# The centring of the next graph's rows moved ahead of the step's closing root, and the four diagonals of E taken by one wide product and one sum

## The reference

```python
h = jnp.maximum(_layernorm(x), 0.0)
def layer(h, params):
    u = einsum('bid,bjd->bij', h, h) / sqrt(D)
    a = softmax(u, axis=-1)
    delta = a * adjacency_matrix
    attn = delta / (sum(delta, axis=-1, keepdims=True) + 1e-10)
    hl, hs, hr = h @ wl.T + b_l, h @ ws.T + b_s, h @ wr.T + b_r
    diag_a = jnp.diagonal(attn, axis1=1, axis2=2)
    ctx = (attn * upper) @ hl + diag_a[..., None] * hs + (attn * lower) @ hr
    o = (ctx - mean(ctx)) / sqrt(var(ctx) + 1e-12) * g + beta
    return relu(o)
out = x + layer(layer(h, params[0]), params[1])
```

## Time and profile before

| what | us |
|---|---|
| median of 3 runs | 1187.16 (1187.15 to 1187.18) |
| the profiled execution | 1188.02 |
| its span, first to last instruction | 1186.3 |
| PE busy | 1169.5 (99%), 6998 matmuls |
| DVE busy | 1004.8 (85%) |
| POOL busy | 633.0 (53%) |
| ACT busy | 494.5 (42%) |

### The profile page before, as it was taken

How to read it: one execution, slowest core, us unless ns; L and a number is a source line. 1 busy time by engine, 2 the same in 40 slices (tenths; PEclk the granted TensorE clock), 3 DMA queues, 4 the chain that set the end, 5 groups by cost and what they waited for, 6 DMA issues and landing times.

```text
span 1186.3 us, 18757 instructions
## 1 busy us (share of the span) xinstructions
PE 1169.5 (99%) x6998; PEld 1157.7 (98%) x6998; DVE 1004.8 (85%) x2064; ACT 494.5 (42%) x1065; POOL 633.0 (53%) x669
## 2 busy tenths in 40 slices
PE   9999999999999999999999999999999999999997
PEld 7999999999999999999999999999999999999997
DVE  6879987799877998779997798977989779895688
ACT  5346423364343543435434343344433454335532
POOL 3676454654545555455564455654556544654347
PEclk9999999999999999999999999999999999999999
DMA  6521312013120131211312112121222113110000
GB/s 226 203 65 54 115 54 81 19 54 116 54 81 19 54 115 55 80 36 55 97 54 81 37 63 90 58 76 37 83 70 80 54 36 104 48 54 1 1 27 27
DMA packets 43483, 80.57 MB, mean 68 GB/s; under 512 B 6912, under 2 KB 24832, under 8 KB 43392
## 3 DMA queue, kind: packets, MB, share of 16 engines
q1 hardware_dynamic: 43104, 78.98, 20.0%
q10 hardware_dynamic: 288, 0.39, 0.1%
HBM read 66.72 MB, written 12.64 MB: 67 GB/s over the span
## 4 chain that ended last, share of the span: by engine, by line
PE 54%; DVE 20%; POOL 10%; issue 10%; ACT 4%; DMA 1%; DVEq 0%; POOLq 0%
PE u_ps L337 9%; PE u_ps L339 9%; PE u_ps L338 9%; PE rot_ps L339 8%; PE rot_ps L338 8%; PE rot_ps L337 8%; POOL dg L957 4%; POOL hw_lo L945 4%; DVE et_lo L682 3%; DVE e_sb L677 3%; DVE xt_sb L665 3%; DVE proj L710 2%; DVE z L747 2%; DVE z L755 2%; ACT e_sb L515 2%
## 5 line engine op out<-in xcount | busy, mean ns | idle before, releaser
L945 POOL TENSOR_TENSOR hw_lo<-proj,hw_hi 128x384 fp32r<-128x384 f32 x256 | 283.1, 1126 | 242.3 <-ACT hw_hi L525 242.3
L337 PE MATMUL rot_ps<-w_hi,ht_hi 128*128 128x384 f32 x1152 | 389.3, 338 | 0.0
L339 PE MATMUL rot_ps<-w_hi,ht_lo 128*128 128x384 f32 x1152 | 385.4, 335 | 0.0
L338 PE MATMUL rot_ps<-w_lo,ht_hi 128*128 128x384 f32 x1152 | 385.2, 334 | 0.0
L338 PEld LDWEIGHTS rot_ps<-w_lo,ht_hi 128*128 128x128 f32 x1152 | 216.6, 188 | 0.0
L337 PEld LDWEIGHTS rot_ps<-w_hi,ht_hi 128*128 128x128 f32 x1152 | 216.5, 188 | 0.0
L339 PEld LDWEIGHTS rot_ps<-w_hi,ht_lo 128*128 128x128 f32 x1152 | 216.3, 188 | 0.0
L500 ACT ACTIVATE u_off<-u_ps 128x128 f32<-128x128 f32 (+1 forms) x128 | 42.4, 332 | 395.6 <-PE u_ps L339 395.4
L525 ACT ACTIVATE hw_hi<-proj 128x384 fp32r<-128x384 f32 x256 | 127.5, 520 | 78.1 <-DVE proj L710 78.1
L957 POOL TENSOR_TENSOR dg<-et_hi,tri 128x256 fp32r<-128x256 f32 x128 | 109.7, 857 | 89.9 <-PE u_ps L339 89.9
L710 DVE TENSOR_TENSOR proj<-rot_ps,bias 128x384 f32<-128x384 f32 x256 | 137.8, 548 | 21.9 <-PE rot_ps L339 21.8
(11 more groups left out here) (89 smaller groups left out, 2100.6 us busy)
## 6 DMA issues: line engine op xcount, KB each, us to landing
out_dram<-z SPq DMA_DIRECT2D x64, 192.0 KB, 1.9
x_norm<-x_dram SPq DMA_DIRECT2D x15, 768.0 KB, 4.5
xt_sb<-x_t_dram SPq DMA_DIRECT2D x15, 768.0 KB, 4.5
adj_a<-adj_t_dram SPq DMA_DIRECT2D x8, 1024.0 KB, 5.3
adj_b<-adj_t_dram SPq DMA_DIRECT2D x8, 1024.0 KB, 5.4
x_norm<-rows_dram SPq DMA_DIRECT2D x15, 512.0 KB, 3.8
x_a<-x_dram SPq DMA_DIRECT2D x8, 768.0 KB, 4.6
x_b<-x_dram SPq DMA_DIRECT2D x8, 768.0 KB, 4.7
```

Source lines behind the costliest of these rows:

```text
L337: pe.matmul(dst, a_hi, b_hi, start=first and m == 0, stop=False)
L338: pe.matmul(dst[:, 0:b_lo.shape[1]], a_hi, b_lo, start=False, stop=False)
L339: done = pe.matmul(dst, a_lo, b_hi, start=False, stop=last and m == n - 1)
L945: pool.tensor_tensor(hw_lo[:, t, n, :], proj[:, t % 2, n, :], hw_hi[:, t, n, 0:dim].bitcast(F32), ALU.subtract).then_inc(hw_lo_done, 1)
```

## The change

Two things are changed. On POOL, `x_centre` stands ahead of `rstd_of` where both occur (s=1 and s=3 of the first seven pairs). On DVE, the four diagonals, which were one fused multiply and sum of 128x128 each, become one product of 128x512 (the four diagonal blocks of E, seen through `diagonal_blocks`, times the identity matrix, broadcast) and one sum of it along the last axis, with a new semaphore `diag_cut` between the two; `finish(0)` now waits for one event of `diag_done` in place of four.

```diff
+        flat_e = e_sb[:, :, :].rearrange("p t n -> p (t n)")
+        diagonal_blocks = flat_e.rearrange("p (b c) -> p b c", c=P)[:, 0:TILES * TILES:TILES + 1, :]
...
-                def diagonal(t):
-                    dve.wait_ge(masked, at(it, s, t + 1, FOUR))
-                    dve.scalar_tensor_tensor(out=diag_junk[:, t, :], in0=e_sb[:, t, t * P:(t + 1) * P],
-                                             scalar=1.0, in1=ident[:, :], op0=ALU.mult, op1=ALU.mult,
-                                             accum_out=e_diag[:, t:t + 1]).then_inc(diag_done, 1)
+                def diagonals():
+
+                    dve.wait_ge(masked, at(it, s, TILES, FOUR))
+                    dve.tensor_tensor(diag_junk[:, :, :], diagonal_blocks, ident[:, :].unsqueeze(1).to_broadcast([P, TILES, P]),
+                                      ALU.mult).then_inc(diag_cut, 1)
+                    dve.wait_ge(diag_cut, at(it, s, 1, ONE))
+                    dve.tensor_reduce(e_diag[:, :], diag_junk[:, :, :], mybir.AxisListType.X, ALU.add).then_inc(diag_done, 1)
...
-                        dve.wait_ge(diag_done, at(it, s, TILES, FOUR))
+                        dve.wait_ge(diag_done, at(it, s, 1, ONE))
...
-                    for t in range(TILES):
-                        diagonal(t)
+                    diagonals()
...
-                rstd_of(slice(0, TILES), 1)
                 if s in (1, 3) and not last:
                     x_centre(it * 2 + (2 if s == 1 else 3))
+                rstd_of(slice(0, TILES), 1)
```

More of the change, by code:

```diff
@@ L145, in build_digcn @@
         masked = sem("masked")
+        diag_cut = sem("diag_cut")
         diag_done = sem("diag_done")
```

## The result

The changed kernel takes 1179.78 us (median of 6 runs, 1179.70 to 1180.04), against 1187.17 before (6 runs, 1187.13 to 1187.80): the ratio is 0.9937, with a 95% interval of 0.9924 to 0.9950. That is 7.4 us less; 6.9 were forecast. The profiled execution has a span of 1178.0 us and took 1179.74.

What follows compares the result with a forecast made beforehand. PE was taken to be the bound, losing time mid-kernel only in two waits repeated seven times. 3.4 + 3.15 + 0.3 = 6.9 us off 1187.16 gave 1180.3 us, range 1178.7 to 1183.9.

Steps and rivals of the forecast that it cites:

- What bounds the kernel: PE's two waits, for hw_lo in s=0 and DVE's evacuation (1, 2) in s=2, seven times each: some 6.6 us.
- s=1 to s=2, 0.45 us a pair: turn_h's wait in s=2 goes, the step taking the last pair's 37.15 us: 7 x 0.45 = 3.15 us.
- s=3 to s=0, 0.48 us a pair: PE's wait in s=0 for POOL's last hw_lo goes: 7 x 0.48 = 3.4 us.
- The root stays in time: In s=1 and s=3 POOL's subtractions end 1.5 to 1.9 us before var_eps, so rstd_of starts as before.
- The head start of more than 2.5 us in s=0: The row of work ahead of hw_lo starts over 2.5 us earlier, otherwise the same; 0.48 us is enough.
- The diagonals: Product and sum take 1.3 to 2.6 us, most likely 1.8; only the last step's tail gains, 0.3 us.
- (a): Rival: only one of PE's two waits goes, the s=2 margin being thin; 1183.5 us, chance 0.14.
- (b): Rival: moved subtractions leave the root and DVE as late as now, only the tail gains; about 1187 us, chance 0.06.
- Rival (c): Wide product takes the port from POOL's last hw_lo in s=0, 0.4 us a pair; 1190.4 us, chance 0.05.
- Rival (d): The single 1.6 us wait in the first pair also goes, DVE reaching x_low sooner; 1178.7 us, chance 0.05.

Runs made afterwards that it cites:

- the last run: Changed kernel with evacuation (1, 2) ahead of e_low(3) in s=2 and s=3, and POOL's first-step split of weights behind the root: 1178.43 us.
- s=1 moved: Kernel before with x_centre ahead of rstd_of in s=1 only: 1183.81 us, ratio 0.9972.
- the second timing: Changed kernel timed again, unaltered, against the kernel before on the same chip: 1180.59 us against 1186.94, ratio 0.9946.
- the dose runs: Changed kernel with six or three memsets added on DVE ahead of the first evacuation of s=0: 1195.42 us with six, 1180.23 with three.
- the diagonals alone: Changed kernel with rstd_of put back ahead of x_centre, so only the diagonals differ from the kernel before: 1188.96 us, ratio 1.0015.
- the root alone: Kernel before with x_centre ahead of rstd_of in s=1 and s=3, four narrow diagonals kept: 1179.78 us; timed again, 1180.40.
- s=3 alone: Kernel before with x_centre ahead of rstd_of in s=3 only: 1183.28 us, ratio 0.9965.

## Why the prediction was right, point by point

- **What bounds the kernel.** Two repeated waits of PE were said to be the whole of what could be gained in the middle. Nearly right: they are gone, and no new one took their place, but the last run found another 0.10 us a pair in s=2, at a place that the list does not show.
- **s=1 to s=2, 0.45 us a pair.** The last pair, without subtractions, served as the measure: 37.15 us forecast, 37.15 measured, and alone (s=1 moved) the same. The `x_scale` took 1.89 us for 1.9. This term was exact since it was read from the kernel itself, not built from durations.
- **s=3 to s=0, 0.48 us a pair.** It measured 0.54. The term was mis-sized by 0.06: I took the distance over the wait, but the first product behind a wait is slower itself (0.41 us in the earlier trace rows, where such a one lasts 0.34), and the next one starts that much later. The usual distance of 0.18 us is not in the earlier trace rows, which the prediction names for it; in the trace it is 0.17 to 0.18. Seven times 0.06 is 0.4 of the 0.5 us by which the forecast fell short. By the traces the sum is 3.8 + 3.1 + 0.3 = 7.2 us; the rest, and the 6.4 us of the second timing, lie within what the start-up moves.
- **The root stays in time.** Forecast were 1.5 to 1.9 us to spare, measured 1.54 in s=3. In s=1 it was more, 2.16: there each subtraction took 1.29 or 1.30 us, while in s=3 two of the three took 1.61 beside a `centre`. In the first pair, where I allowed for a root 1.3 us late, it still waited 0.46. The blocked `centre` cost 0.3 us of DVE, in idle time, as supposed.
- **The head start of more than 2.5 us in s=0.** The first evacuation came 3.15 us earlier (0.80 behind the mirror, not 3.95), the first `mask` waited for ACT as forecast. The row of work was not "otherwise the same": its end, POOL's last `hw_lo`, came only 2.3 us earlier (16.89 for 19.20; 16.62 with the narrow diagonals). The rows did not show how much was needed; the dose runs do: 0.54 us at the end of the row, about 0.75 at its head.
- **The diagonals.** The handover cost under 0.1 us, the sum 0.69 (forecast 0.75), the product 1.17 on average where I had 0.68 free and 1.04 beside POOL. It usually meets one of POOL's instructions: 25 of the 32 started during one and ended 0.55 us behind its end. That the two together still cost 1.86 us, for 1.8 forecast, is luck in part: the product took more than assumed, the sum less. The tail moved by 0.25 to 0.3 us in the traces, as forecast, but the times do not resolve it.
- **Rivals (a) and (b).** Neither came: both waits are gone, and the root still starts as soon as `var_eps` is there.
- **Rival (c), the port.** It had 0.05 and did not decide, but its mechanism is real, at 0.24 us a pair for the 0.4 allowed (the 0.4 is right for the two `hw_lo` alone, 2.45 for 2.05, but the narrow diagonals cost POOL something behind them), and the condition stated for it (no head start in s=0) is what separates the diagonals alone, 1.65 us slower, from the changed kernel. My theory for that run forgot it: there I wrote 1185.8 to 1186.9, with the port as the rival.
- **Rival (d), the first pair.** Its wait for `ht_lo` fell from 1.6 to 0.5 us and makes the profiled span fall by 8.3 us, not 7.4. It is not shown to be an effect of the change, and the same kernel does it by itself: the changed kernel's first step took 36.03 us in one trace and 36.56 in the other, the root alone 36.03 and 36.70; before it was 37.21, with s=3 alone 37.60, and 36.99 and 37.65 in the two runs with memsets on DVE. It follows the landing of the second load of rows that the statistics (`x_stats`) read: started 1.1 to 1.2 us ahead of the first mirror, they go with a first step of 36.03 us, 0.55 ahead with 36.56, 0.15 ahead with 36.70, 0.4 behind it with 37.21. The two rows are DVE's timeline before and, under it, after:

```profile
18.93 1.94 DVE L610 BATCH_NORM_STATS2 x_stats<-x_norm 128x6 f32<-128x384 f32 x4 [3.36 <-DMA x_norm<-x_dram]
```

```profile
17.46 1.94 DVE L615 BATCH_NORM_STATS2 x_stats<-x_norm 128x6 f32<-128x384 f32 x4 [1.76 <-DMA x_norm<-x_dram]
```

## What to carry to other kernels

When the busiest engine waits at the same place in every turn, follow the waited-for row of work back to its head, and look there for POOL work that reads SBUF beside DVE work with two SBUF operands; POOL's idle time ahead of an instruction that it must wait for anyway is the place to put such work. A turn of the loop that lacks the suspected work (here the last pair) priced the change better than the sums of durations did. Fewer and wider instructions are not free where another engine's work has to wait for them: the wide product saves DVE about 1 us a step and still made the kernel slower where POOL was the one waited for.

## What the runs showed that I had not expected

- Less work on DVE made the kernel slower (1.0015, 1.0006 to 1.0024): one product of 128x512 stretched two `hw_lo` of POOL from 1.97 to 2.45 us; beside the four narrow ones these two took 2.05.
- Eight memsets of POOL, 4.61 us in all, left DVE's two-operand instructions at their free durations (1.15 us for two), while three subtractions of 3.66 us in all made these 2.70.
- The loss has a threshold: a first evacuation 3.2 us behind the mirror costs PE 0.06 us a pair, one 3.95 us behind it 0.54, and one 4.75 us behind it 2.03. Counted by the end of POOL's last `hw_lo`, each microsecond beyond the threshold costs one.
- The start-up, where a landing of the first loads decides, moved the first step between 36.03 and 37.65 us among kernels that hardly differ there, and by 0.5 and 0.7 us between two traces of one kernel; a difference of a microsecond in one profiled execution says nothing by itself.
